# A two-layer kernel on one Trainium2 core: loads and gate logits moved into the feed-forward, the bound check into the last group, the second norm onto ACT tile by tile, expert weights loaded earlier

## What is computed

```python
# layer 0, feed-forward: FP4 fake-quantized gate/up/down (352 wide)
h = silu(q(x) @ q(w_gate).T) * (q(x) @ q(w_up).T);  x += q(h) @ q(w_down).T
# layer 0, recurrent attention, 16 heads of 64, on hs = normed x
q, k, v = silu(hs @ Wq + bq), silu(hs @ Wk + bk), silu(hs @ Wv + bv)
beta, fd, sd, fg, sg = (sigmoid(hs @ W + b) for five 128x16 gate weights)
S_f, S_s = two 64x64 states per head, decayed, delta-rule updated, capped if their norm is over 64
o = fg * (q @ S_f) + sg * (q @ S_s)
x += (rmsnorm(o) * onorm_w * g) @ Wo + bo
# layer 1, on xn = layernorm(x): 16-head causal attention (head width 8) and a top-1 mixture of 8 experts
x += softmax(causal(q k^T / sqrt(8))) v @ Wp + bp
x += top_prob * (silu(xn @ W1[e] + b1[e]) @ W2[e] + b2[e])      # e = argmax of the gate
```

## Time and profile before

| | us |
|---|---|
| three runs: median (lowest, highest) | 3439.89 (3428.99, 3453.76) |
| profiled execution: its time, its span | 3432.23, 3430.6 |

### The profile page before, as it was taken

One profiled execution on the slowest core, in us unless ns is written; L12 is line 12 of the kernel. 1 busy time (PEld: TensorE's weight loads), 2 busy tenths in 40 slices (PEclk: granted clock), 3 DMA queues, 4 the chain that ended last, 5 costly groups with the idle time before them and its releaser, 6 DMA issues. The chain is left out here.

```text
span 3430.6 us, 74926 instructions
## 1 busy us (share of the span) xinstructions
PE 2858.1 (83%) x28151; PEld 1973.1 (58%) x28151; DVE 2554.0 (74%) x4553; ACT 1598.3 (47%) x3575; POOL 1238.9 (36%) x1882
## 2 busy tenths in 40 slices
PE   0565999685999999999999999999484459998888
PEld 0343544364777777777777777777372443333323
DVE  8897588794787868787787868766597347777775
ACT  1222799784344444444444444434252335555554
POOL 0000233312565656666565656655464230000000
PEclk9876999896999999999999999999697779999999
DMA  1001465686123132323323232222472521011111
GB/s 31 0 0 52 166 246 234 256 259 162 34 74 68 38 83 64 78 44 74 67 71 56 53 83 63 66 45 64 148 259 75 157 60 20 20 29 20 20 26 27
DMA packets 487658, 290.81 MB, mean 85 GB/s; under 512 B 402907, under 2 KB 447515, under 8 KB 478493
## 3 DMA queue, kind: packets, MB, share of 16 engines
q1 hardware_dynamic: 478080, 256.61, 27.5%
q10 hardware_dynamic: 4608, 16.78, 1.6%
q0 software_dynamic: 4608, 12.59, 1.1%
HBM read 155.92 MB, written 129.97 MB: 83 GB/s over the span
## 5 line engine op out<-in xcount | busy, mean ns | idle before, releaser
L2388 DVE TENSOR_REDUCE mx<-banks 128x2 f32<-128x1024 f32 (+3 forms) x384 | 358.2, 955 | 146.0 <-PE banks L1839 95.2
L2080 ACT ACTIVATE probs<-banks 128x1024 f32<-128x1024 f32 (+3 forms) x384 | 309.9, 810 | 257.1 <-PE banks L1864 143.8
L1116 ACT COPY xs<-banks 64x64 f32<-64x64 f32 (+2 forms) x640 | 166.2, 260 | 397.9 <-PE banks L958 394.8
L828 POOL TENSOR_SCALAR xc<-xc,halves 128x64 f32<-128x64 f32 (+1 forms) x256 | 193.9, 757 | 359.4 <-DVE xc L1299 346.5
L958 PE MATMUL banks<-xc,ssm 64*64 64x16 f32 (+2 forms) x5120 | 249.9, 217 | 37.1 <-issue 35.0
L958 PEld LDWEIGHTS banks<-xc,ssm 64*64 64x64 f32 x5120 | 209.7, 135 | 116.4 <-issue 57.7
L1718 PE MATMUL banks<-wproj,xnT 128*128 128x512 f32 x512 | 265.4, 600 | 0.9 <-DVE sb_tok L2165 0.9
L1589 POOL TENSOR_TENSOR prj_sq<-prj 128x1024 f32<-128x1024 f32 x32 | 77.6, 2424 | 490.7 <-ACT prj L1983 490.7
L1299 DVE SCALAR_TENSOR_TENSOR xc<-xc,halves,banks 64x64 f32<-64x64 f32 (+1 forms) x512 | 160.0, 312 | 110.8 <-PE banks L969 104.7
L1106 ACT COPY ssm<-banks 16x64 f32<-16x64 f32 (+2 forms) x896 | 215.9, 241 | 50.4 <-PE banks L930 38.3
L1141 ACT COPY ah<-banks 128x768 f32<-128x768 f32 x128 | 102.2, 798 | 254.4 <-PE banks L990 254.4
(11 more groups left out here) (352 smaller groups left out, 6744.7 us busy)
## 6 DMA issues: line engine op xcount, KB each, us to landing
proj_s<-prj SPq DMA_DIRECT2D x32, 2048.0 KB, 6.7
qkv_t<-proj_s SPq DMA_DIRECT2D x32, 1536.0 KB
ka<-proj_s ACTq DMA_DIRECT2D x32, 512.0 KB, 4.5
mem_s<-o_sb SPq DMA_DIRECT2D x32, 512.0 KB, 2.6
om<-mem_s SPq DMA_DIRECT2D x32, 512.0 KB, 3.8
om<-proj_s SPq DMA_DIRECT2D x32, 512.0 KB, 4.8
nblk_s<-ssa POOLq DMA_DIRECT2D x32, 256.0 KB, 4.2
blk_s<-res SPq DMA_DIRECT2D x16, 512.0 KB, 4.3
```

The lines of the kernel that those rows point to most:

```text
L828: pool.tensor_scalar(inverse_of(k, lv + 1)[:, :, w:2 * w], inverse_of(k, lv), halves[:, lv, 1:2], None, ALU.mult).then_inc(half_set, 1)
L1116: last = act.copy(xs[right, k % 2, 0:4 * (SUB << lv)], products(k, lv, out_)[right, :])
L2080: act.activation(probs[:, s % 2, :, at:at + w], slot_of((kind, s, k))[:, :, 0:w], ACT.Exp, scale=D1 ** -0.5).then_inc(b_read, 1)
L2388: dve.tensor_reduce(mx[:, s % 2, c, :, t:t + 1].rearrange("p e a -> p (e a)"), slot_of((kind, s, k))[:, :, 0:w], AX, ALU.max).then_inc(a_r ...
```

## The change

- Feed-forward: SP issues all of the projections' loads right behind the feed-forward's own. PE makes the gate logits of each pair right after `gate_up` of that pair, into the free bank 5, once as rows (256 columns) and once, for beta alone, token by token; ACT copies both out after `signs`. At p = 14 DVE waits until the last of these copies is done, adds the beta bias and the gate bias, and ACT takes Sigmoid of all and the root of beta. The bias split is 5 operations on POOL on all 128 partitions, with a store to DRAM and a load back. The stage of its own between the feed-forward and the projections is gone.
- Bound check: the sums of squares are kept in another order, PE makes them in the needed layout by 16 small matmuls in the last round of the loop, between `answers` and `values0` of the last group, and DVE runs the check there too, ahead of `put_output`. No DRAM round trip, one `end_phase` less. Wo (one DMA), bo and onorm_w are loaded, and wout scaled, in the last groups.
- Second norm: per tile on ACT inside the output stage, 5 to 7 rounds behind: a Copy with accumulation, a multiplication of the sum, an Identity with the negative mean as bias, a Square with accumulation; DVE multiplies by 1/std in 8 groups afterwards. The semaphores are cleared at the head of the output stage, `q_parts`, `k_parts` and `mxz` are zeroed by POOL between the tiles 4 to 13.
- Expert weights are loaded at the end of the output stage. `parts` has 4 buffers in place of 8. The add of bp to `res` (L2341) moves behind the splits. `load_pairs(0)` is issued in 12 parts during the experts.

The diff, cut to its core:

```diff
+        fc_top = fc[:, T * D - NW:T * D]
...
+        rest = o_all[:, 0:2 * TB, :].rearrange("p (n t) d -> p n (t d)", n=2)
...
+            sp.wait_ge(av_mm, GROUPS - 4)
+            sp.wait_ge(kc_set, GROUPS - 4)
+            sp.wait_ge(cv_set, GROUPS - 4)
+            sp.dma_start(wout, a["Wo"].rearrange("(c p) d -> p c d", p=P)).then_inc(ld4, 16)
+            sp.dma_start(bout, a["bo"].partition_broadcast(P)).then_inc(ld4, 16)
+            for e in range(2):
+                sp.dma_start(onw[DK * e:DK * e + DK, :], a["onorm_w"].rearrange("(d a) -> d a", a=1)).then_inc(ld4, 16)
...
-            for e in range(2):
-                for b in range(B):
-                    sp.dma_start(bn0[64 * e:64 * e + 64, b, :], nrm_s[e, TB * b:TB * b + TB, :].rearrange("c (h j) -> h c j", j=2)).then_inc(nrm_in, 16)
...
+            pool.wait_ge(ld4, 64)
+            pool.tensor_scalar(wout, wout, onw, None, ALU.mult).then_inc(wout_set, 1)
...
+            def state_norms():
+
+                pe.wait_ge(sq_set, later(GROUPS - 1))
+                pe.wait_ge(o_set, GROUPS - 1)
+                pe.wait_ge(s_new, GROUPS - 1)
+                for b in range(B):
+                    for j in range(2):
+                        for e in range(2):
+                            last = pe.matmul(bank[0][64 * e:64 * e + 64, 2 * b + j:2 * b + j + 1], sqr[:, b, j, :, :].rearrange("p h c -> p (h c)"), half[:, e:e + 1],
+                                             start=True, stop=True)
+                last.then_inc(nrm_mm, 1)
...
+                if old and not new:
+                    state_norms()
...
-            act.copy(nrm_sb[:, :, :].rearrange("p t h -> p (t h)"), bank[0][0:2, 0:T * H0]).then_inc(nrm_set, 1)
-            end_phase(act)
-            act.wait_ge(nrm_in, 16 * 2 * B)
-            act.activation(bnx[:, :, :], bn0[:, :, :], ACT.Sqrt).then_inc(bn_root, 1)
...
+            def check_bound():
+
+                dve.wait_ge(bn_root, 1)
+                dve.wait_ge(bx_set, 3 + 5 * P)
+                dve.wait_ge(g_mm2, GROUPS)
+                wide4 = [P, 2 * P, B]
+                cols3 = bx[:, 1:P + 1, :, :, :].rearrange("p t j c b -> p (t j) c b")
+                for j in range(2):
+                    seq.link(dve.tensor_tensor(bh[:, j], cols3[:, :, j, :], bnx[:, :, j].unsqueeze(1).to_broadcast(wide4), ALU.mult))
+                seq.link(dve.tensor_tensor(bh[:, 0], bh[:, 0], cols3[:, :, 2, :], ALU.add))
+                seq.link(dve.tensor_tensor(bh[:, 0], bh[:, 0], bh[:, 1], ALU.add))
+                seq.link(dve.tensor_scalar(bh[:, 0], bh[:, 0], BOUND, None, ALU.is_le))
+                dve.tensor_reduce(bmin[:, :], bh[:, 0].rearrange("p t b -> p (t b)"), AX, ALU.min).then_inc(bmin_set, 1)
...
+                if not new:
+                    check_bound()
...
+            sp.dma_start(beta_row[:, :], a["bgate"][0:H0, :].rearrange("h a -> (h a)").partition_broadcast(P)).then_inc(ld2, 16)
+            sp.dma_start(bias_p[:, :], a["bproj"].rearrange("a (p n) -> (a p) n", p=P)).then_inc(ld2, 16)
+            for n, w in enumerate(("Wq", "Wk", "Wv", "Wg")):
+                sp.dma_start(wproj[:, HD * n:HD * n + HD], a[w]).then_inc(ld2, 16)
+            sp.wait_ge(bias_split, 5)
+            sp.dma_start(bias_s.rearrange("c (p n) -> p c n", p=P), bias_h[:, :, :]).then_inc(bias_out, 16)
+            sp.wait_ge(bias_out, 16)
+            sp.wait_ge(bias_set, 2)
+            sp.dma_start(bias3[0:3, :], bias_s).then_inc(bias_in, 16)
+            end_phase(sp)
+
+            sp.wait_ge(g_done, 1)
...
+            sp.dma_start(wall[:, :, 0:HID], a["W1"].rearrange("e p n -> p e n")).then_inc(wall_in, 16)
+            for e in range(E1):
+                sp.dma_start(wall[:, e, HID:2 * HID].rearrange("p (c d) -> p c d", d=D), a["W2"][e].rearrange("(c p) d -> p c d", p=P)).then_inc(wall_in, 16)
+            sp.dma_start(wall[:, :, 2 * HID:2 * HID + HID // P], a["b1"]).then_inc(wall_in, 16)
+            sp.dma_start(wall[:, :, WROW - D:WROW], a["b2"].partition_broadcast(P)).then_inc(wall_in, 16)
+            end_phase(sp)
...
-            sp.wait_ge(lo_set, 2 * B)
...
-            load_pairs(0)
...
+                if j == 8:
+                    for n in range(4):
+                        sp.wait_ge(parts_out[n], 96)
+                    sp.wait_ge(qk_init, 10)
+                if 8 <= j < 20:
+                    load_pairs(0, [j - 8])
...
+            pool.wait_ge(xq_done, 1)
+            pool.memset(bias3[:, :], 0.0).then_inc(bias_set, 1)
+            pool.wait_ge(ld2, 144)
+            split = Count(pool, bias_split)
+            split.link(pool.tensor_copy(bias_h[:, 0, :], bias_p[:, :]))
+            split.link(pool.tensor_tensor(bias_r[:, 0, :], bias_p[:, :], bias_h[:, 0, :], ALU.subtract))
+            split.link(pool.tensor_copy(bias_h[:, 1, :], bias_r[:, 0, :]))
+            split.link(pool.tensor_tensor(bias_r[:, 1, :], bias_r[:, 0, :], bias_h[:, 1, :], ALU.subtract))
...
+                if 4 <= i < 8:
+                    pool.memset(q_parts[:, i % 2, i // 2 % 2, :], 0.0).then_inc(qk_init, 1)
+                elif 8 <= i < 12:
+                    pool.memset(k_parts[:, i % 2, i // 2 % 2, :], 0.0).then_inc(qk_init, 1)
+                elif 12 <= i < 14:
+                    pool.memset(mxz[:, i % 2, :, :], 0.0).then_inc(mask_set, 1)
...
+            def gate_logits(p):
+
+                if p == 0:
+                    pe.wait_ge(ld2, 144)
+                else:
+                    pe.wait_ge(g_raw, 2 * p)
+                pe.matmul(bank[5][0:5 * H0, 0:2 * P], wgate[:, :], xnT[:, 2 * P * p:2 * P * p + 2 * P], start=True, stop=True)
+                for y in range(2):
+                    at = 2 * P + H0 * y
+                    last = pe.matmul(bank[5][:, at:at + H0], xnT[:, 2 * P * p + P * y:2 * P * p + P * y + P], wgate[:, 0:H0], start=True, stop=True)
+                last.then_inc(g_mm, 1)
...
-            pe.wait_ge(norm_done, 2)
-            pe.wait_ge(mask_set, 11)
+            pe.wait_ge(ld5, 80)
             for g in range(T // 4 + 1):
                 if g < T // 4:
...
+            def keep_logits(p):
+                act.wait_ge(g_mm, p + 1)
+                act.copy(gates[:, 2 * P * p:2 * P * p + 2 * P], bank[5][0:5 * H0, 0:2 * P]).then_inc(g_raw, 1)
+                act.copy(sb_tok[:, 2 * p:2 * p + 2, :].rearrange("p t h -> p (t h)"), bank[5][:, 2 * P:2 * P + 2 * H0]).then_inc(g_raw, 1)
...
+                if p == FP - 2:
+                    act.wait_ge(g_raw, 2 * FP)
+                    act.wait_ge(g_bias, 1)
+                    act.activation(gates[:, :], gates[:, :], ACT.Sigmoid, bias=bgate[:, 2:3]).then_inc(g_done, 1)
+                    act.wait_ge(b_summed, 1)
+                    act.activation(sb_tok[:, :, :], sb_tok[:, :, :], ACT.Sigmoid).then_inc(g_done, 1)
+                    act.wait_ge(g_done, 2)
+                    act.activation(sb_tok[:, :, :], sb_tok[:, :, :], ACT.Sqrt).then_inc(sb_root, 1)
...
+                if 6 <= i < T + 6:
+                    j = i - 6
+                    act.wait_ge(ln_sum, j + 1)
+                    act.mul(stats[:, 1, j:j + 1], stats[:, 0, j:j + 1], -1.0 / D).then_inc(ln_mean, 1)
+                if 5 <= i < T + 5:
+                    j = i - 5
+                    act.wait_ge(o_added, j + 1)
+                    act.activation(ln_out[:, 0, :], res[:, j, :], ACT.Copy, accum_out=stats[:, 0, j:j + 1]).then_inc(ln_sum, 1)
+                if i >= 7:
+                    j = i - 7
+                    act.wait_ge(ln_centred, j + 1)
+                    act.activation(ln_out[:, 1, :], xn1[:, j, :], ACT.Square, accum_out=stats[:, 2, j:j + 1]).then_inc(ln_var, 1)
+                if 6 <= i < T + 6:
+                    j = i - 6
+                    act.wait_ge(ln_mean, j + 1)
+                    act.activation(xn1[:, j, :], res[:, j, :], ACT.Identity, bias=stats[:, 1, j:j + 1]).then_inc(ln_centred, 1)
...
+                if p == FP - 2:
+                    dve.wait_ge(g_raw, 2 * FP)
+                    dve.tensor_tensor(sb_tok[:, :, :], sb_tok[:, :, :], beta_row[:, 0:2 * H0:2].unsqueeze(1).to_broadcast([P, T, H0]), ALU.add).then_inc(b_summed, 1)
+                    dve.wait_ge(ld2, 144)
+                    dve.tensor_tensor(bgate[:, 2:3], bgate[:, 0:1], bgate[:, 1:2], ALU.add).then_inc(g_bias, 1)
...
+            dve.wait_ge(ln_var, T)
+            dve.tensor_scalar(stats[:, 1, :], stats[:, 2, :], 1.0 / D, LN_EPS, ALU.mult, ALU.add).then_inc(var_done, 1)
+            dve.wait_ge(std_done, 2)
+            seq.link(dve.reciprocal(stats[:, 2, :], stats[:, 0, :]))
...
-            layernorm(dve, seq, res, xn1, xnT1, 1)
+            for g in range(T // 4):
+                four = xn1[:, 4 * g:4 * g + 4, :]
+                dve.tensor_tensor(four, four, stats[:, 2, 4 * g:4 * g + 4].unsqueeze(2).to_broadcast([P, 4, D]), ALU.mult).then_inc(norm_done, 1)
...
```

247 lines of the change are left out of this document (100 added, 147 removed).

## The result

| | before | after |
|---|---|---|
| median of 4 runs each (lowest, highest), us | 3442.8 (3428.99, 3453.76) | 3355.22 (3348.59, 3360.27) |
| profiled execution, its time and span | 3432.23, 3430.6 | 3356.96, 3355.3 |

The ratio is 0.9746, with a 95% interval of 0.9706 to 0.9787. Two later comparisons, on other chips, gave 0.9759 (0.9743 to 0.9775) and 0.9750 (0.9732 to 0.9768). The forecast was 3359, the range 3338 to 3388. It was counted from a median of 3439.9 for the kernel before; with a fourth run that median is 3442.8, so the gain is 87.6 us where 81.1 were forecast.

The account below looks back on a forecast made before the run. Stretches between busy stages, where engines wait for one another by turns, were the target: -34.3 - 14.4 + 2 - 27 - 7.4 = -81.1 from 3432.2 gives 3351.1, plus 7.7 to the median, say 3359 us; range 3338 to 3388.

Parts of the forecast that it names:

- Gates: Feed-forward's end to projections: -34.3 us, from -39.0 for the removed stage, +3.7 DVE's wait at p = 14, +1 PE's logits.
- Bound check: Last loop round to the first og: -14.4 us, bounds -15.9 and -10.5, with 3 us taken for the norms' matmuls.
- Output stage: Tiles of the output stage: +2 us, bounds 0 and +10, as ACT's four operations leave 0.25 us in two tiles.
- Second norm and routing: Last add to last logits: -27 us, from 47.05 to 20, bounds -30 and -20.
- what is late next is POOL: Second norm: POOL's masks start after the meeting and the value copies wait for them, until +8.5 us.
- Splits and scatters: First scatter to first expert matmul: -7.4 us, from 62.9 to 55.5, bounds -9 and -4.
- SP was last: Before the experts, SP asked for xst at 2699.60, behind weights and 24 pair loads; the last scatter was issued at 2689.66.
- 1 (PE bounds the pairs): Feed-forward: PE stays at 1.2 GHz, each pair costs 1.1 us more, +16 on the forecast, 3375; chance 0.10.
- 2 (loads delay the value copies by 15): Second norm: expert weights meet om and small loads, value copies start 15 us later, +23, 3374; chance 0.12.
- 3: DVE's wait at p = 14, last-round matmuls and ACT's four operations at upper bounds: +4, +4, +8, 3375; chance 0.06.
- 4: Output stage: ACT reloads its function table, two loads a tile 3434 us, four 3516; chances 0.03 and 0.02.
- 5: The change doesn't do what it says, since the stages were hidden anyway; within 1% of before; chance 0.02.

Follow-up runs that it names:

- the three later kernels: The changed kernel with four, six and eight further edits at head, pairs, second norm and scatters; ratios to the kernel before 0.9722, 0.9694 and 0.9701.
- the kernel with four edits: Changed kernel with bias3 cleared later, split remainders in PSUM, bias sums on POOL, only vaug's ones column set; 3337.05 against 3351.35 us.

## Why the prediction was right, point by point

The time lies in the range, and for each of the four stretches the wait that was to go did go. Without the loop and the attention the stages give -86.0 where the sum says -81.1; no step is off by more than 3.6 us, but some sizes came out right by errors that cancelled, as is said below.

- **Gates.** -39.0 was -39.1, DVE's stall 3.2 (forecast 3.7), and the pairs took nothing from PE's logits where +1 was entered: 200.3 + 3.2 is the whole of 203.5. The slack at the low clock was sized from one pair; four times the logits cost 4.6 us in all.
- **What the sum left out: +3.2 at the head.** The step that failed is the pricing of the bias split: the prediction counts the bias as "done earlier" and gives POOL's memset of `bias3` and its five operations no price. POOL was idle there, but not free: DVE's operation waited for POOL's memset, and POOL's small ones for DVE's. The earlier trace rows had shown a like thing, `gated` and `og` by turns (2.07 us, of which 1.2 run after gated has ended). The rule of the Trainium skill that names this case (SBUF — State Buffer, Who interferes with whom) says that a DVE `tensor_scalar` in a two-port mode and any GpSimd operation exclude one another for the whole instruction. The traces agree: 4.06 us beside the memset and 0.74 without it; which mode the operation ran in, no view shows.
- **Bound check.** -14.5 against -14.4 is in part luck. In the three traces of the changed kernel this stage took 35.4, 32.8 and 37.2 us, so its gain lies between 12.7 and 17.1 against the one trace of before. And two errors cancelled: the 32 records took 1.2 us (entered 3, with a lower bound of 1.5 that no row gives), and from the end of the last output to the first om load it was 6.8 us (entered 4.2), of which 3.0 are DVE's late record behind the branch, 0.5 before.
- **Output stage.** -1.6 against +2: a tile stayed at 3.59. ACT's four operations took the 1.0 a tile of the forecast (1.08 from the start of the first to the end of the last), but the slack beside them was some 0.4 a tile, not 0.12. The 1.6 gained lie at its start, where `wout` no longer holds POOL for 7.05 us.
- **Second norm and routing.** First turn at +4.2 (3.6, whose terms add to 3.5), value copies at +8.7 (8.5), last logits at +18.1 (20): the groups went at 1.37 us each as entered, and the first two overlapped the wait. The step "what is late next is POOL" was right but not alone: the load, DVE's own multiplications and PE stood within about a microsecond of it, as the three later kernels showed one after another.
- **Splits and scatters.** -8.3 against -7.4. The end was worked out from what is last now, the scatters, and that held: 51.0 us of issuing, 1.3 until SP asks for the slots, 2.3 to the matmul, where 50.2, 2.5 and 2.8 were entered (the 2.5 without a row). "SP was last" held too, but of what took SP off the path the prediction names only the weights and pairs, which stand for 1.5 of the 8.3 us; the earlier start of the splits gave 4.5 and the wait for the stores, now behind the weights, 2.1. And "The add of bp stays 4.4 us beside a scatter, just later" priced the collision at nothing, as before and after alike. Alike it is (10.0 and 10.7 us of issuing lost to DVE), but before it was hidden, and now it is the stage's length.
- **Rivals.** 1 (PE bounds the pairs) was far off: even four times the logits cost 4.6 us and not 16. 2 (loads delay the value copies by 15) did not come: in the kernel with four edits, POOL's masks out of the way, a load ended last, at +9.1, which is 0.4 behind them and not 15. 3 did not come; the three terms it names stayed below its bounds. 4: no table load stands in the output stage; the two in the feed-forward, 1.28 each, are hidden, as is the Exp's behind the meeting. 5: no.

## What to carry to other kernels

Before work is given to an idle POOL, list what DVE runs at that moment. Three pairings cost time here: POOL's memset with a DVE `tensor_scalar` (0.74 us became 4.06), a POOL operation that reads SBUF with a DVE operation that has two inputs there (1.82 became 2.78), and POOL's issue of an indirect DMA with a DVE operation of two SBUF inputs or a copy there (0.96 became 1.9 to 4.0 and 1.2 to 1.6), which a row of such DMAs pays at each meeting. Where a wait is taken away behind a meeting of the engines, look for all that ends within a microsecond of it, since the gain stops at the second. A stage's end is best worked out from what is last after the change; how much each edit gives is another question, and here the smaller moves gave more than the one that was aimed at the wait.
